# Feed-forward products of a four-stage network: three half-precision terms of split operands in place of one float32 product

## The reference, cut to what matters

```python
def _mx_dequant(t):                       # blocks of 32 along the last dimension
    max_abs = jnp.max(jnp.abs(blocks), axis=-1)
    scales = jnp.maximum(max_abs / 448.0, 1e-30)
    q = (blocks / scales[..., None]).astype(jnp.float8_e4m3fn).astype(jnp.float32)
    return (q * scales[..., None]).reshape(rows, feat)

def _mx_linear(x2d, w):
    return _mx_dequant(x2d) @ _mx_dequant(w).T

gate = _mx_linear(x2d, gate_w)            # 256 -> 1024
up = _mx_linear(x2d, up_w)                # 256 -> 1024
h = jax.nn.silu(gate) * up
out = _mx_linear(h, down_w)               # 1024 -> 256
```

## Time and profile before

| | |
|---|---|
| median of three runs | 659.71 us |
| profiled execution, its own time | 655.62 us |
| span in its trace (first to last instruction) | 653.8 us |
| TensorE busy | 540.6 us (83% of the span) |
| VectorE busy | 411.6 us (63%) |
| GpSimd busy | 307.6 us (47%) |
| ScalarE busy | 248.4 us (38%) |
| mean granted TensorE clock | 0.957 |

### The profile page before, as it was taken

The page is one execution under the profiler, slowest core; times in us unless marked ns, Lnnn a source line. Parts: engine busy times, 40 slices in busy tenths (PEclk is TensorE's granted clock), DMA queues, the critical chain, the costliest instruction groups (busy, mean ns, idle before and its releaser), DMA issues.

```text
span 653.8 us, 8556 instructions
## 1 busy us (share of the span) xinstructions
PE 540.6 (83%) x3032; PEld 339.6 (52%) x3032; DVE 411.6 (63%) x806; ACT 248.4 (38%) x674; POOL 307.6 (47%) x300
## 2 busy tenths in 40 slices
PE   2862676868797679899999899999997999999696
PEld 1752334545454557555555575555554766554442
DVE  3999793479667536976864569768644353534244
ACT  1842221232433223543344334433442245354143
POOL 3765344259739713263345532542455224345466
PEclk9985898899999799999999998999998999999799
DMA  7940100012202200000000000000000000000000
GB/s 288 408 146 14 51 0 5 1 65 97 97 33 97 90 0 21 1 5 1 2 1 1 17 1 2 1 2 1 0 1 1 17 2 2 1 1 1 17 1 16
DMA packets 10201, 24.56 MB, mean 38 GB/s; under 512 B 4464, under 2 KB 6512, under 8 KB 9264
## 3 DMA queue, kind: packets, MB, share of 16 engines
q1 hardware_dynamic: 9920, 23.24, 9.9%
q0 software_dynamic: 240, 0.79, 0.3%
HBM read 22.97 MB, written 1.05 MB: 37 GB/s over the span
## 4 chain that ended last, share of the span: by engine, by line
PE 52%; DVE 27%; POOL 7%; ACT 6%; issue 6%; DMA 1%; SPq 0%; POOLq 0%; DVEq 0%; ACTq 0%
PE s L512 13%; PE qc L512 11%; PE ga L512 10%; PE qb L512 10%; PE ua L512 6%; DVE wk L1062 4%; DVE top L1060 3%; PE tp L515 2%; ACT reg L857 2%; DVE amax L987 2%; DVE reg L1134 2%; POOL reg L1375 2%; DVE nmax L1141 2%; POOL wE L1421 1%; DVE masks L1212 1%
## 5 line engine op out<-in xcount | busy, mean ns | idle before, releaser
L1375 POOL TENSOR_TENSOR reg<-reg,rsum 128x512 f32<-128x512 f32 x64 | 68.3, 1089 | 129.7 <-DVE rsum L1148 129.7
L857 ACT ACTIVATE reg<-s,nmax 128x256 f32<-128x256 f32 x128 | 59.0, 476 | 45.8 <-DVE nmax L1141 45.8
L1212 DVE SCALAR_TENSOR_TENSOR masks<-s,route,masks 128x256 f32<-128x256 f32 x120 | 51.5, 477 | 38.5 <-PE s L512 38.3
L512 PE MATMUL s<-wE,xhi 128*128 128x512 fp8e4 x192 | 73.6, 383 | 1.3 <-ACT reg L857 0.9
L512 PE MATMUL s<-wE,xlo 128*128 128x512 fp8e4 x192 | 73.5, 383 | 0.0
L512 PE MATMUL qc<-reg,wM 128*64 128x256 f32 (+1 forms) x384 | 68.6, 396 | 2.8 <-DVE reg L1134 2.8
L515 PE MATMUL tp<-idn,reg 128*128 128x128 f32 x248 | 39.8, 283 | 31.8 <-POOL reg L1375 16.0
L512 PE MATMUL qb<-reg,wA_hi 128*128 128x256 f16 x384 | 64.6, 278 | 1.5 <-ACT reg L842 1.4
L779 ACT COPY reg<-tp 128x512 f32<-128x512 f32 (+1 forms) x56 | 32.0, 572 | 67.8 <-PE tp L515 67.8
L1141 DVE TENSOR_REDUCE nmax<-s 128x2 f32<-128x512 f32 x64 | 40.9, 680 | 22.7 <-PE s L512 22.7
L512 PEld LDWEIGHTS qc<-reg,wM 128*64 128x64 f32 (+1 forms) x384 | 37.2, 153 | 31.6 <-issue 21.8
(11 more groups left out here) (192 smaller groups left out, 1094.6 us busy)
## 6 DMA issues: line engine op xcount, KB each, us to landing
masks<-in_moe_masks SPq DMA_DIRECT2D x16, 512.0 KB, 3.3
wM<-in_att_wq SPq DMA_DIRECT2D x1, 2048.0 KB, 7.7
wE<-in_wo_t SPq DMA_DIRECT2D x1, 2048.0 KB, 11.2
reg<-in_kc_q SPq DMA_DIRECT2D x1, 1536.0 KB, 10.9
reg<-in_qr_t SPq DMA_DIRECT2D x1, 1536.0 KB, 18.3
xb<-in_x SPq DMA_DIRECT2D x4, 256.0 KB, 3.4
wU<-in_gate_w SPq DMA_DIRECT2D x1, 1024.0 KB, 12.9
wD<-in_up_w SPq DMA_DIRECT2D x1, 1024.0 KB, 14.9
```

The costliest lines, as they stand in the source:

```text
L512: return nc.tensor.matmul(dst, lhsT, rhs, start=start, stop=stop, skip_group_check=not check)
L857: nc.scalar.activation(attn[p % 2][:, k * S:(k + 1) * S], s.tensor[:, (k % 2) * S:(k % 2 + 1) * S], ACT.Exp, bias=nmax[:, o:o + 1], accum_ ...
L1212: ins = nc.vector.scalar_tensor_tensor(acc[:, t, chain], src, w, acc[:, t, chain], ALU.mult, ALU.add)
L1375: nc.gpsimd.tensor_tensor(a, a, rsum[:, o + 2 * hh:o + 2 * hh + 2].unsqueeze(2).to_broadcast([P, 2, S]), ALU.mult).then_inc(attn_ready.sem, 1)
```

## The change

Every operand of the feed-forward products is stored as two half-precision tensors, the value rounded to float16 and the remainder, and each product becomes three half-precision products summed in the same bank: high by high, high by low weight, low by high weight. Weights are scaled by 64 and hidden values by 16, and the factors are taken out in instructions that were there already.

```diff
-                for k, w in ((GA, wG), (UA, wU)):
+                for m, k in enumerate((GA, UA)):
                     pe.wait_ge(k.drained, k.free(key))
                     for c in range(C):
-                        last = mm(k.tensor[:, :], xqT[...], w[...], c == 0, c == C - 1)
+                        for i, (x, w) in enumerate(((xqT_hi, w_hi[m]), (xqT_hi, w_lo[m]), (xqT_lo, w_hi[m]))):
+                            last = mm(k.tensor[:, :], x[...], w[...], c == 0 and i == 0, c == C - 1 and i == 2)
...
                 for j in range(I // P):
-                    last = mm(GA.tensor[:, 0:D], hqT[...], wD[...], j == 0, j == I // P - 1)
+                    for i, (x, w) in enumerate(((hqT_hi, w_hi[2]), (hqT_hi, w_lo[2]), (hqT_lo, w_hi[2]))):
+                        last = mm(GA.tensor[:, 0:D], x[...], w[...], j == 0 and i == 0, j == I // P - 1 and i == 2)
```

On the activations ScalarE's copy writes the high part, and a new VectorE instruction reads PSUM and subtracts. The bank is freed by VectorE now, where ScalarE freed it before:

```diff
             def hidden_turn(b, t):
-                drain(GA, ("hidden_turn", b, t), hqT[:, 0:512], GA.tensor[:, :])
-                drain(UA, ("hidden_turn", b, t), hqT[:, 512:1024], UA.tensor[:, :])
+                for i, k in enumerate((GA, UA)):
+                    act.wait_ge(k.filled, k.done(("hidden_turn", b, t)))
+                    nc.scalar.copy(hqT_hi[:, i * 512:(i + 1) * 512], k.tensor[:, :]).then_inc(hq_hi_ready.sem, 1)
...
+            def in_low(b):
+                dve.wait_ge(xq_hi_ready.sem, xq_hi_ready.at(b, 1))
+                low(xqT_lo, UA.tensor[:, :], xqT_hi).then_inc(UA.drained, 1)
+
+            def hidden_low(b, t):
+                for i, k in enumerate((GA, UA)):
+                    dve.wait_ge(hq_hi_ready.sem, hq_hi_ready.at(b, 2 * t + i + 1))
+                    low(hqT_lo[...], k.tensor[:, :], hqT_hi[...]).then_inc(k.drained, 1)
```

On the weights ScalarE writes a high part and a full copy of each of the twelve transposed pieces (two instructions for one), and GpSimd subtracts. The full copies go round four buffers:

```diff
+            def weights_low(m):
+                for n in range(4):
+                    i, k = 4 * m + n, bank_of("turn_w", m, n)
+                    pool.wait_ge(w_hi_ready.sem, i + 1)
+                    pool.wait_ge(k.drained, k.done(("turn_w", m, n)))
+                    nc.gpsimd.tensor_tensor(w_lo[m][...], w_full[i % 4], w_hi[m][...],
+                                            ALU.subtract).then_inc(w_lo_ready.sem, 1)
...
                 dequant_w(m)
                 if m == 0:
                     rstd(0, 1)
+                    weights_low(0)
             ffn_in(0)
+            weights_low(1)
             dequant_w(2)
+            weights_low(2)
             for t in range(T):
                 ffn_up(0, t)
```

```diff
-    6: ([('ffn_up', 3)], [('round', 1, 0)], [('round', 1, 1)], [], [('ffn_down', 0)]),
-    7: ([], [], [], [], [('ffn_down', 1)]),
+    6: ([('ffn_up', 3)], [('round', 1, 0)], [('round', 1, 1)], [('hidden_low', 0)], [('ffn_down', 0)]),
+    7: ([], [], [], [('hidden_low', 1)], [('ffn_down', 1)]),
```

More of the change, by code:

```diff
@@ L31 @@
 EF = 4
+W_UP, H_UP = 64.0, 16.0
 EPS = 1e-5
@@ L149 @@
     3: ([], [], [], [('ffn_in',)], []),
-    4: ([], [], [('ffn_up', 0)], [], [('ffn_up', 1), ('round', 0, 0)]),
+    4: ([], [], [('in_low',), ('ffn_up', 0)], [], [('ffn_up', 1), ('round', 0, 0)]),
     5: ([], [('round', 0, 1), ('ffn_up', 2)], [], [], [('ffn_up', 3)]),
-    6: ([], [('round', 1, 0)], [('round', 1, 1)], [], []),
-    7: ([], [], [], [('ffn_down', 0)], [('ffn_down', 1)]),
+    6: ([], [('round', 1, 0)], [('round', 1, 1)], [('hidden_low', 0)], []),
+    7: ([], [], [], [('ffn_down', 0), ('hidden_low', 1)], [('ffn_down', 1)]),
 }, {
@@ L158 @@
     3: ([('adjacency_out',)], [], [], [('ffn_in',)], []),
-    4: ([], [], [('ffn_up', 0)], [('ffn_up', 1)], [('round', 0, 0)]),
+    4: ([], [], [('in_low',), ('ffn_up', 0)], [('ffn_up', 1)], [('round', 0, 0)]),
     5: ([], [('round', 0, 1), ('ffn_up', 2)], [], [], []),
-    6: ([('ffn_up', 3)], [('round', 1, 0)], [('round', 1, 1)], [], [('ffn_down', 0)]),
-    7: ([], [], [], [], [('ffn_down', 1)]),
+    6: ([('ffn_up', 3)], [('round', 1, 0)], [('round', 1, 1)], [('hidden_low', 0)], [('ffn_down', 0)]),
+    7: ([], [], [], [('hidden_low', 1)], [('ffn_down', 1)]),
 }]
@@ L302, in build @@
         hid, qy, qm, hq = (ffn[:, i * I:(i + 1) * I] for i in range(4))
-        hqT = ffn[:, 4096:5120]
+        hqT_hi, hqT_lo = (ffn[:, o:o + I // 2].bitcast(F16) for o in (4096, 4608))
         xn = ffn[:, 5120:5632]
-        xqT = ffn[:, 5632:6144]
+        xqT_hi, xqT_lo = (ffn[:, o:o + C * S // 2].bitcast(F16) for o in (5632, 5888))
+        w_hi, w_lo = ([w[:, h * I:(h + 1) * I].bitcast(F16) for w in (wG, wU, wD)] for h in range(2))
         sg = sb("sg", 512)
@@ L353, in build @@
         wA_full = [ffn[:, 2048:2816], ffn[:, 2816:3584]]
+        w_full = [reg[:, 1024 + 512 * i:1536 + 512 * i] for i in range(4)]
         wscale = [wsc[:, 0:64], wsc[:, 64:128]]
@@ L608, in ffn_up @@
                 if b == 0 and u == 0:
-                    pe.wait_ge(GA.drained, GA.done(("turn_w", 1, 2)))
-                for k, w in ((GA, wG), (UA, wU)):
+                    pe.wait_ge(w_lo_ready.sem, 8)
+                for m, k in enumerate((GA, UA)):
                     pe.wait_ge(k.drained, k.free(key))
                     for c in range(C):
-                        last = mm(k.tensor[:, :], xqT[:, c * S + t * P:c * S + (t + 1) * P],
-                                  w[:, c * I + half * 512:c * I + (half + 1) * 512], c == 0, c == C - 1)
+                        for i, (x, w) in enumerate(((xqT_hi, w_hi[m]), (xqT_hi, w_lo[m]), (xqT_lo, w_hi[m]))):
+                            last = mm(k.tensor[:, :], x[:, c * S + t * P:c * S + (t + 1) * P],
+                                      w[:, c * I + half * 512:c * I + (half + 1) * 512], c == 0 and i == 0, c == C - 1 and i == 2)
                     last.then_inc(k.filled, 1)
@@ L825, in ffn_in @@
             def ffn_in(b):
-                drain(UA, ("ffn_in", b), xqT, UA.tensor[:, :])
+                act.wait_ge(UA.filled, UA.done(("ffn_in", b)))
+                nc.scalar.copy(xqT_hi, UA.tensor[:, :]).then_inc(xq_hi_ready.sem, 1)
             def ffn_up(b, u):
@@ L980, in _, with quantise @@
         def _(dve):
-            def quantise(step, q0, free, f0, src, dst, mag, scale, blocks, part=None):
+            def quantise(step, q0, free, f0, src, dst, mag, scale, blocks, part=None, floor=1e-30):
                 def blk(ap):
@@ L1026, in quantise_hidden @@
                 n = 1 + t
-                quantise(q_step, q_step.at(b, 8 * n), hq_ready, hq_ready.at(b, n), hid, qy, qm, qsc[:, 0:32], 32, part)
+                quantise(q_step, q_step.at(b, 8 * n), hq_ready, hq_ready.at(b, n), hid, qy, qm, qsc[:, 0:32], 32, part,
+                         1e-30 * H_UP)
                 if part != 0:
@@ L1229, in _ @@
                     ffn_in(0)
+            in_low(0)
             for u in range(4):
@@ L1234, in _ @@
             for t in range(T):
+                hidden_low(0, t)
                 ffn_down(0, t)
@@ L1260, in _ @@
                 steps = {"top": top_rounds, "masked": masked, "adjacency_out": adjacency_out, "ffn_in": ffn_in,
-                         "ffn_up": ffn_up, "round": quantise_hidden, "ffn_down": ffn_down}
+                         "ffn_up": ffn_up, "round": quantise_hidden, "ffn_down": ffn_down,
+                         "in_low": in_low, "hidden_low": hidden_low}
                 for p in range(PAIRS):
```

28 lines of the change are left out of this document (20 added, 8 removed).

## The result

The changed kernel takes 693.97 us (median of 4 runs, 690.81 to 695.58) against 659.44 us before (656.06 to 660.26): a ratio of 1.0528, 95% interval 1.0470 to 1.0585. It is slower, as forecast, but by 34.5 us instead of 17, outside the range given. The profiled execution took 690.81 us, its span is 689.0, the mean granted clock 0.905.

The account below looks back on a forecast made before the run. TensorE held 52% of the chain of waits, VectorE 27%. Setup +5.5, pass 0 -0.5 and twice +6.2 for passes 1 and 2 gave +17.4 us, so 676 us, range 665 to 686.

Parts of the forecast that it names:

- Products: Feed-forward on TensorE: `ffn_up` bank from 1.72 to 1.30 us, `ffn_down` from 3.45 to 2.76; 4.8 us gained per feed-forward.
- Passes 1 and 2, steps 4 and 5: Cheaper `ffn_up` products, less new waits, gain 2.2 us at the scores of step 6; ends 1.2 and 3.4.
- Step 6 and the clock: Passes 1 and 2: `ffn_down(0)` stalls 7.6 us behind `hidden_low(0)`, the clock falls; each pass loses 6.2, 2.4 of it clock.
- Pass 0: Pass before the two with experts: gains and later down products nearly cancel, -0.5 us; ends -2 and +1.5.
- Setup: Stage before the passes, with twelve new GpSimd subtractions: +5.5 us; ends +2.5 and +9.
- The first four subtractions: Setup, GpSimd: at 1.12 us each they fill its 4.68 us wait before 59.88 and cost nothing.
- The late `in_low` and the cold first product: Setup: `in_low(0)` comes late and the first gate product runs at the lower clock; +2 us, ends 0.7 and 4.
- Scaling of hidden tile 0: Setup, GpSimd: stands behind the last four subtractions, near 101 instead of 92.42, 8.7 us late, not all paid.
- Then keys, 5.3 us: Setup, GpSimd: keys lie between the scalings of tiles 0 and 1, putting the latter's end at 110.1 against 103.15, +7 us.
- more than forecast: Rival: half-precision pieces no faster than float32, or GpSimd subtractions taking 2 us; 10 us more, 686 us; chance 0.08.
- the clock did not stay up: Rival it answers: the stall comes but the clock stays up, 12.6 us slower, 672 us; chance 0.15.
- the setup was not hidden: Rival it answers: setup hidden or nearly so, as keys and scaling shrink beside quiet VectorE; 673 us, chance 0.15.

Follow-up runs that it names:

- e_low_early: Changed kernel with VectorE's two subtractions for hidden tile 0 moved ahead of the second rounding part of tile 1 in all three passes; 675.33 us, ratio 1.0269.
- e_warm2: Changed kernel with 56 unneeded products ahead of both waits of the first down product in passes 1 and 2; 688.10 us, ratio 1.0449.
- e_combo: Changed kernel with the moves of e_low_early and e_pool2, and the setup's `hidden_low(0)` between the rounding parts of tile 1; 664.89 us, ratio 1.0104.
- e_warm: Changed kernel with 56 unneeded products behind the first wait of the first down product in passes 1 and 2, setup and pass 0 unedited; 702.14 us, ratio 1.0682.
- e_pool2: Changed kernel with the setup's last four GpSimd subtractions (down matrix) moved behind the scaling of hidden tile 0; 689.17 us, ratio 1.0475.
- e_up_neg2: Changed kernel with float32 down product, TensorE and ScalarE replacing GpSimd's subtractions, gate/up weights turned by identity products; low parts lack the remainder; 650.08 us, ratio 0.9888.
- e_up_neg3: e_up_neg2 with the start mark on only the first of a bank's four turning products, no end marks; leaves nothing out; 650.94 us, ratio 0.9900.

## Why the prediction was right in kind and wrong in size

**Products.** Right. A bank of `ffn_up` is 1.29 us start to start (rows 340.35 and 341.64 of TensorE below), and the down product at full clock 2.6, a little less than the 2.76 of the sum.

```profile
340.35 1.46 PE L519 MATMUL ga<-wG,ffn 128*128 128x512 f16 x6
341.64 1.46 PE L519 MATMUL ua<-wU,ffn 128*128 128x512 f16 x6
```

**Passes 1 and 2, steps 4 and 5.** Right. From the first row maxima of the pass (rows below, before and after) to the reciprocal of step 6, 83.2 us became 81.0, a gain of 2.2 as forecast; in pass 2 it is 2.5.

```profile
254.01 1.25 DVE L1141 TENSOR_REDUCE nmax<-s 128x2 f32<-128x512 f32 x2
```

```profile
276.33 1.25 DVE L1168 TENSOR_REDUCE nmax<-s 128x2 f32<-128x512 f32 x2
```

**Step 6 and the clock.** Right. From that reciprocal to the last addition, 23.6 us became 32.3 in pass 1 and 31.7 in pass 2. The forecast was 2.2 + 6.2 = 8.4 more, measured 8.7 and 8.0. e_low_early shows the place as the cause, e_warm2 gives the clock its share.

**Start of pass 1.** Not in the sum. The first row maxima come 26.0 us behind the last addition of pass 0, 23.6 before: +2.4. TensorE's clock over 250 to 260 is 0.72 after; before it was 1.00 over 230 to 240. In pass 2 both take 24.4. This 2.4 is nearly all of the 2.6 by which pass 1 missed. I priced a stall's low clock only on the product behind it, not on the next stage's start. What lowers it there stays open. e_low_early and e_combo run the same instructions from pass 0 on, and from 12 us before the end of pass 0 to 4 us behind it TensorE has the same waits in both (6.28, 0.64, 0.72 and 1.70 us). Yet from the last addition to the first row maxima it is 26.0 us in the first and 23.5 in the second.

**Pass 0.** Near, and partly by luck: +1.3 against ends of -2 and +1.5, where the same instructions took up to 3.9 us more in e_warm. TensorE's row in it after the change:

```profile
238.93 5.28 PE L519 MATMUL ga<-wD,ffn 128*128 128x256 f16 x24 [7.26 <-DVE ffn L1137]
```

I gave this product 4.5 us, and its record is 5.28 long, at the lower clock.

**Setup.** This is the step that failed: +18.6 where "I take +5.5", ends 2.5 and 9. It had one cost at nothing that was 4.9 us, and the wrong path to the end of the stage: over GpSimd's keys, where it ran over VectorE's two waits. By its parts:
- "The first four subtractions fill the 4.68 us for which GpSimd waited before 59.88, the next four the wait for the down matrix: nothing." The first four took 8.57 us, not 4.5, so the scaling at 59.88 moved to 63.46, and the rounding on VectorE slowed beside all eight: 4.9 us. Counted from VectorE's first product on the up matrix it is 5.2, of which 3.1 came by the end of that scaling and 2.1 beside the next four. My 1.12 holds where VectorE is quiet (1.15), not beside VectorE's products of two inputs, where one took 3.2. The prediction named the rule on the shared ports (the Trainium skill, GPSIMD Engine Reference, Specifications) and put 2 us on it, outside the sum. The trace agrees with the rule for the two products of two inputs (3.27 and 3.12 us for 2.29), and the price is more than twice as high. Instructions of one input were slowed too: beside the next four subtractions one of 128x64 took 1.17 us for 0.20 and one of 128x2048 2.06 for 1.23. The row of the skill names VectorE's two-port mode as a second case, which the prediction left out; whether these ran in it, no run here shows.
- The late `in_low` and the cold first product: 2.1 us (the last gating is 7.0 late, 4.9 of it from above); I took 2. Right.
- Scaling of hidden tile 0 behind the last four: forecast "near 101", measured 106.58. I followed it to GpSimd's own later work alone. VectorE's quantisation of tile 1 has a wait on that scaling as well, and stood 6.72 us. The scaling of tile 1 then started at 114.96 and not at about 108. e_pool2 returned 5.4 us.
- `hidden_low(0)` behind the rounding of tile 1 in the setup: I saw this order in the loop and missed it in the code of the setup. The down product of tile 0, forecast nowhere as a stall, waited 5.66 us and took 5.24 at the lower clock. Together with the subtraction of tile 1 that is the last 4.9 us of 18.6. e_combo, with both moves, ended the setup 8.5 earlier, 3.1 of it beyond e_pool2.
- "Then keys, 5.3 us" put them on the path. They took 3.3 us (108.44 to 111.75) and were not on it: the scaling of tile 1 waited another 3.21 us for VectorE.

So of the rivals "more than forecast", with its subtractions of 2 us, came nearest, at a chance of 0.08 and 686 us. The first four subtractions did take 2.1 us each, but they and the next four cost the 4.9 us above, not 10. The two overlooked waits, with what hung on them, are 11.6 us (6.7 and 4.9). Of the others, the clock did not stay up, and the setup was not hidden.

Left open: what sets the clock at the start of a pass. It is no property of the order alone. e_up_neg2 and e_up_neg3 differ in marks of products only, yet from the end of the setup to the first row maxima they take 18.1 and 19.8 us. The changed kernel takes 18.6 and e_warm 20.5 in the same stretch of the same instructions. So the 23.0 us of e_combo may be its order or its execution, and no run tells.

## What to carry to other kernels

When a cheaper instruction comes with helper work on a second engine, ask of each helper what stands ahead of it in that engine's program, in every copy of the loop and in the setup too: here moving the same subtraction ahead of a rounding took more than 6 us off each of passes 1 and 2. Follow a late step to every wait on its semaphore, not only to what is next on its own engine. And an idle gap of one engine is not free room for work that reads the same memory as its neighbour; TensorE and ScalarE had such room here, and e_up_neg3 used it. And before a difference of a few us in one stage is put down to an edit, look for another run that executes this stage unchanged: here pass 0 moved by 3.9 us without one.

## What the runs showed of the hardware

- A VectorE instruction of one input can stand beside a GpSimd instruction until that ends. In e_up_neg3 a scale of 128x16 takes 3.12 us, from 60.59 to 63.71, while GpSimd's scaling runs from 60.04 to 63.68 (row below; in the kernel before it was so too). After the change the scaling began later, at 63.46, and the delay fell on another: 128x512 took 3.75 us, from 64.08 to 67.83, with GpSimd's end at 67.54. So this wait was there before the change too, and the change lengthened it by less than half a us. The same instruction takes 0.43 alone. The two were never tried apart from the rest of the setup.

```profile
60.04 3.64 POOL L1354 TENSOR_TENSOR wD<-wD,wsc 128x2048 f32<-128x2048 f32 x1 [4.68 <-DVE wD L1055]
```

- With two inputs from SBUF on both sides, both slow: VectorE's 128x2048 product from 2.29 to 3.27 us, GpSimd's subtraction from 1.15 to 2.14 on average, 3.20 at most.
- A product that starts an accumulation marks more than its own columns. With the mark on all four 128-column products of a bank (e_up_neg2) a following product without it did not add to all of them; with the mark on the first alone (e_up_neg3, where the end marks of the four are gone too) it did. The Trainium skill (PSUM — Partial Sum Buffer, Terms) says that such a product clears the state of the whole bank in the partitions that it writes; the two kernels agree with it. Their times are within 0.2% of each other.
